# An attention block on one core: cosine product ahead of the block transposition in one step, a set-up product spread over two

## What is computed

```python
xn = layernorm(x)
# attention of xn, with its own norm h = layernorm(xn) * scale + bias
c_q, c_kv = h @ w_down_q.T, h @ w_down_kv.T            # latents, 64 wide
q, k = rope(heads(c_q @ w_up_q.T)), rope(heads(c_kv @ w_up_k.T))
v = heads(c_kv @ w_up_v.T)
attn = softmax(q @ k.T / 8)
a = merge(attn @ v) @ w_out.T + xn
# spiking feed-forward part of xn
y = square(relu(xn @ W_fc.T)) @ W_proj.T
f = (number of 5 leaky integrate-and-fire steps in which y makes the neuron fire) / 5
out = x + a + f
```

## Time and profile before

| | us |
|---|---|
| median of 3 runs | 1083.32 (1083.18 to 1086.99) |
| profiled execution, its own time | 1083.63 |
| its span, first to last instruction | 1081.8 |
| mean granted TensorE clock | 0.993 of full |
| busy: TensorE matmul | 1041.4 (96%) |
| busy: ScalarE | 930.0 (86%) |
| busy: VectorE | 898.9 (83%) |
| busy: GpSimd | 895.9 (83%) |
| DMA engines, mean busy share | 76% |

### The profile page before, as it was taken

The page is one execution under the profiler, slowest core; times in us unless marked ns, Lnnn a source line. Parts: engine busy times, 40 slices in busy tenths (PEclk is TensorE's granted clock), DMA queues, the critical chain, the costliest instruction groups (busy, mean ns, idle before and its releaser), DMA issues.

```text
span 1081.8 us, 26191 instructions
## 1 busy us (share of the span) xinstructions
PE 1041.4 (96%) x6880; PEld 700.7 (65%) x6880; DVE 898.9 (83%) x1223; ACT 930.0 (86%) x3136; POOL 895.9 (83%) x897
## 2 busy tenths in 40 slices
PE   3789999999999999999999999999999999999987
PEld 2556666666666666666666666666666666666654
DVE  3798888898888889888889888889888888888872
ACT  3789988988998888999898999898899889898861
POOL 3777989888888888888898888988888988888851
PEclk9899999999999999999999999999999999999999
DMA  5388777877877877777887777787777787777773
GB/s 178 106 227 207 204 209 202 223 211 200 205 208 204 230 203 207 206 202 202 219 215 207 203 203 209 201 228 208 199 208 206 203 229 204 210 195 196 207 193 81
DMA packets 93281, 217.96 MB, mean 201 GB/s; under 512 B 22464, under 2 KB 43200, under 8 KB 93120
## 3 DMA queue, kind: packets, MB, share of 16 engines
q1 hardware_dynamic: 92864, 216.52, 75.5%
q10 hardware_dynamic: 384, 1.05, 0.4%
HBM read 7.77 MB, written 4.19 MB: 11 GB/s over the span
## 4 chain that ended last, share of the span: by engine, by line
PE 80%; issue 6%; DVE 6%; SPq 3%; ACT 2%; DMA 2%; ACTq 0%; DVEq 0%; POOL 0%; POOLq 0%
PE ps_s L328 20%; PE ps_u L342 20%; PE ps_b L447 10%; PE ps_qk L318 8%; PE ps_a L383 5%; PE ps_a L396 5%; PE ps_qk L319 4%; SPq L254 3%; PE ps_b L413 2%; DVE turned L703 2%; DVE qk L687 2%; PE ps_a L355 1%; PE ps_a L360 1%; PE ps_b L456 1%; PE ps_a L367 1%
## 5 line engine op out<-in xcount | busy, mean ns | idle before, releaser
L538 ACT ACTIVATE prob<-ps_s,neg_max 128x256 f32<-128x256 f32 x1024 | 475.0, 486 | 41.0 <-DVE neg_max L692 38.2
L837 POOL TENSOR_TENSOR partner<-partner,rope_sb 128x512 f32<-128x512 f32 x256 | 327.1, 1278 | 108.3 <-DMA partner<-raw 108.3
L692 DVE TENSOR_REDUCE neg_max<-ps_s 128x4 f32<-128x1024 f32 x256 | 310.8, 1214 | 116.9 <-PE ps_s L328 115.4
L840 POOL TENSOR_TENSOR qk<-qk,partner 128x512 f32<-128x512 f32 x256 | 326.5, 1275 | 20.1
L703 DVE STREAM_TRANSPOSE turned<-prob 128x1024 f32<-128x1024 f32 x256 | 316.4, 1236 | 2.3 <-ACT prob L538 1.3
L328 PE MATMUL ps_s<-qk 64*128 64x256 f32 x2048 | 292.4, 404 | 3.5 <-ACT prob L538 2.4
L342 PE MATMUL ps_u<-gathered,ckv 128*64 128x256 f32 x2048 | 278.4, 393 | 3.1 <-DMA gathered<-turned 2.8
L328 PEld LDWEIGHTS ps_s<-qk 64*128 64x128 f32 x2048 | 177.5, 187 | 106.0 <-issue 86.5
L538 ACT ACTIVATION_READ_ACCUMULATOR prob<-ps_s,neg_max 128x1 f32 x1024 | 221.8, 217 | 0.0
L550 ACT COPY raw<-ps_qk 128x512 f32<-128x512 f32 x256 | 154.1, 602 | 67.0 <-PE ps_qk L319 66.9
L342 PEld LDWEIGHTS ps_u<-gathered,ckv 128*64 128x64 f32 x2048 | 124.8, 136 | 107.8 <-issue 52.6
(11 more groups left out here) (67 smaller groups left out, 897.5 us busy)
## 6 DMA issues: line engine op xcount, KB each, us to landing
gathered<-turned SPq DMA_DIRECT2D x1016, 128.0 KB, 2.4
partner<-raw SPq DMA_DIRECT2D x256, 256.0 KB, 2.4
x_sb<-in_x SPq DMA_DIRECT2D x32, 128.0 KB, 2.3
resid<-early SPq DMA_DIRECT2D x32, 128.0 KB, 2.0
out<-out_sb SPq DMA_DIRECT2D x32, 128.0 KB, 2.1
turned<-in_wup SPq DMA_DIRECT2D x2, 512.0 KB, 5.7
gathered<-turned ACTq DMA_DIRECT2D x8, 128.0 KB, 4.0
rope_sb<-in_rope SPq DMA_DIRECT2D x1, 512.0 KB, 6.8
```

The lines of the kernel that those rows point to most:

```text
L538: last = nc.scalar.activation(prob[:, s % 2, :, h, :, t, :].rearrange("p j k c -> p k j c"), ps_s[:, s % 2, h, t, :].rearrange("p (k j c) ...
L692: nc.vector.tensor_reduce(neg_max[:, s % 2, :, :], ps_s[:, s % 2, :, :, :], AXIS_X, ALU.max, negate=True).then_inc(max_ready, 1)
L837: nc.gpsimd.tensor_tensor(other, other, sin_sb, ALU.mult).then_inc(sin_ready, 1)
L840: nc.gpsimd.tensor_tensor(qk[:, s % 4, :, :], qk[:, s % 4, :, :], other, ALU.add).then_inc(rope_done, 1)
```

## The change

VectorE: in the step p = 1 of every batch, and there alone, `rotate` stands in front of `turn`; `split_latents` stays behind both. TensorE: `value_by_output` takes the half as an argument and is called at p = 6 (pairs 0 to 3, into `ps_u`) and at p = 7 (pairs 4 to 7, into `ps_b`) of b = -2, instead of as a whole at p = 7. ScalarE's copy waits for both halves. The instructions are the same in number and form.

```diff
-            def value_by_output():
+            def value_by_output(half):
                 pe.wait_ge(w_later, LATER_LOADED)
-                for half in range(2):
-                    for j in range(PAIRS // 2):
-                        pair = half * PAIRS // 2 + j
-                        for h in range(2):
-                            rows = slice(h * DH, (h + 1) * DH)
-                            last = nc.tensor.matmul((ps_u, ps_b)[half][h * L:(h + 1) * L, j * D:(j + 1) * D],
-                                                    wv_sb[rows, pair, :], wo_sb[rows, pair, :],
-                                                    start=True, stop=True)
+                for j in range(PAIRS // 2):
+                    pair = half * PAIRS // 2 + j
+                    for h in range(2):
+                        rows = slice(h * DH, (h + 1) * DH)
+                        last = nc.tensor.matmul((ps_u, ps_b)[half][h * L:(h + 1) * L, j * D:(j + 1) * D],
+                                                wv_sb[rows, pair, :], wo_sb[rows, pair, :],
+                                                start=True, stop=True)
                 last.then_inc(setup_pe, 1)
...
-                if p == 7 and isinstance(b, int) and b == -2:
-                    value_by_output()
+                if p in (6, 7) and isinstance(b, int) and b == -2:
+                    value_by_output(p - 6)
...
-                act.wait_ge(setup_pe, 1)
+                act.wait_ge(setup_pe, 2)
...
-                if not outside(g + LEAD["turn"], STEPS):
+                if p != 1 and not outside(g + LEAD["turn"], STEPS):
                     turn(g + LEAD["turn"], s + LEAD["turn"], i)
                 if not outside(g + LEAD["project"], STEPS):
                     rotate(g + LEAD["project"], s + LEAD["project"])
+                if p == 1 and not outside(g + LEAD["turn"], STEPS):
+                    turn(g + LEAD["turn"], s + LEAD["turn"], i)
                 if p == 1 and not outside(b + 2, B):
                     split_latents(b + 2, b0)
```

## The result

The changed kernel is slower, as forecast: 1098.11 us median of four runs (1096.35 to 1100.01) against 1083.71 (1083.18 to 1086.99), ratio 1.0127 with a 95% interval of 1.0100 to 1.0153. The profiled execution took 1096.35 us, its span is 1094.5. Lines of VectorE and ScalarE have a number one lower than before (L686 is the cosine product, L702 the transposition, L730 the split of the latents, L549 the copy to `raw`), and so has TensorE's product of the weights (L465), since the diff takes out a line above them.

The account below looks back on a forecast made before the run. TensorE's full queue was taken as the bound. 1083.6 us plus 13.2 (14 even batches x 0.55 = 7.7, 15 odd x 0.37 = 5.5) plus 0 at the start gave 1096.8 us; own range 1091 to 1102, widened to 1086 to 1104.

Parts of the forecast that it names:

- The bound: TensorE's queue, steady part: once a batch L318 stalls 0.14 us; L396, waiting for the split, starts at 0.38 not 0.23.
- The order, steady part: VectorE at p = 1: waiting for the raw copy delays split and L396, 0.55 us even, 0.37 odd; 13.2 us together.
- the product's hold of the queue: VectorE at p = 1: the cosine product holds the queue 0.57 us before the transposition can start.
- The idle time that I gave as a sign: VectorE in front of the cosine product at p = 1: idle 0.59 us (even) and 0.37 us (odd), waiting for raw.
- The split waits for the full transposition: VectorE at p = 1: the split starts only after the transposition's full end, 1.27 us after its start.
- The lower bound: VectorE at p = 1: if split and transposition overlap, delay is 0.11 us smaller per batch; total cost 7.5 us.
- Nothing accumulates, everything behind shifts alike: Steps behind L396: row maximum, exponentials and next product come 0.59 us later, TensorE too, so no further stall.
- The start: Pipeline fill: halves bring scores(0) 1.1 us sooner, the reorder makes the split 1.1 us late; net 0, -1.4 to +1.1.
- The sum: Whole kernel: profiled 1083.6 us plus 13.2 in the steady batches plus 0 in the fill gives 1096.8 us.
- Rival 1: TensorE at L318 and L396: L396 not held by the split, so the projection's stall goes; 1078 us, chance 0.08.
- Rival 2: ScalarE's raw copy: comes earlier once TensorE is later, VectorE waits only some 0.15 us; 1088 us, chance 0.12.
- Rival 3: Projection of p = 3: stalls 0.43 us more because the product of p = 2 is late; 1109 us, chance 0.10.

Follow-up runs that it names:

- third experiment: Against the kernel before: VectorE at p = 1 runs cosine product, split, transposition, weight products in one block; 1097.54 us, ratio 1.0127.

## Why the prediction was right, point by point

- **The bound.** Right: a stall of 0.14 us at L318 and a second gap at L396 behind the split. That L396 hung on the split already was the step that decided, and it held: before and after, L396 starts 0.05 to 0.13 us behind the split's end, and with the split moved forward it stands 0.23 us behind L413, undisturbed (third experiment).
- **The order, steady part.** Right in mechanism and place. Per pair of batches I had 0.55 + 0.37 = 0.92 us, measured are 1.02 to 1.04. TensorE's own distances give the same: L396 is 0.77 and 0.55 us later behind L413, and L318 0.15 and 0.14 us sooner behind the scores, together 1.03. The term that was too small is the product's hold of the queue: an instruction that VectorE starts out of a wait ran 0.69 us and was followed after 0.61 (584.68 - 584.07), where I took 0.57 from a product that had not waited. That is 0.04 us a batch, twice a pair. The idle time that I gave as a sign, 0.59 and 0.37 us, came out as 0.51 and 0.29: it counts from the end of the row maximum, and I had counted from the start of the transposition, which overlaps its end by 0.08 to 0.09. The delay is not touched by it.
- **The split waits for the full transposition.** Right: 585.95 - 584.68 = 1.27 us. The lower bound, with the overlap of 0.08 us, would have missed by 0.11 us a batch. The Trainium skill (VectorE: DVE Perf Modes, Two Vector instructions with no wait between them) says that an instruction whose output starts in another group of 32 partitions than the last output to the same memory is held until all earlier ones have finished. The trace agrees: the split, which writes from partition 64 on first, came 1.27 us behind the start of the transposition with its 1.24 us.
- **Nothing accumulates, everything behind shifts alike.** Right: one step on, L318 stands 590.07 - 589.00 = 1.07 us behind the scores in the changed kernel's timeline, and every pair is the same.
- **The start.** Right for these two executions: the copy 1.04 us sooner for 1.1, the split 0.1 us later for 0. The halves themselves took 1.90 us (21.29 to 23.19) and 1.26 us (25.20 to 26.46), for 1.62 and either 0.97 or 1.62. I had read the 0.97 as the higher clock; the stretch view gives a granted clock of 1.00 for both halves before (24.92 to 26.54 and 26.54 to 27.51), so that rests on the pace alone. This pace differs from one execution to the next: in the traces of this case scores(0) starts at 27.51 to 28.40 us with the products in one block, and at 25.55 to 26.62 with the halves. The kernel before was profiled at the early end of its range, so 1.05 us is near the low end of what the halves give, and that it met my 1.1 is in part luck. The parts alone show both terms, weakly: the order alone is slower than the whole change by 0.0021 in ratio (2.3 us, with intervals that overlap), the halves alone faster than before by 0.001.
- **The sum.** From the first steady split to the last, 995.58 to 1010.13, the changed kernel is 14.55 us late, of which 0.94 us are there at the first (95.59 to 96.53). I had 13.2: short by the product's hold, about 1.2 us, and by 0.3 us in the fill (the second split, 65.20 for 64.89). The span grew by only 12.7. The last stretch gave back 1.85 us; the granted clock there was 0.97 in the profile before and 1.00 in that after (stretch view, the last lines of before and of after, below), so part of it may belong to the two executions profiled and not to the change; the other three runs were 1.4 to 3.7 us above the profiled one. The clock alone does not explain it: the halves alone, with VectorE's order as before, had a granted clock of 1.00 for 70 us behind their last split, and their last stretch took 86.59 us all the same, where the kernel before took 86.22 and the changed one 84.37. I had no term for it, and it stays open. So my 1096.8 stands as near to the profiled 1096.35 by luck, since two errors of opposite sign cancel; the medians lie 14.4 us apart, where I had 13.2.

```profile
1000.00:1082.00 82.00, 71.68 (x444) 46.03 (x442) 49.28 (x66) 46.36 (x155) 43.16 (x40) 0.97 0.62 160
```

```profile
1000.00:1095.00 95.00, 84.49 (x542) 54.50 (x540) 61.88 (x81) 59.82 (x203) 55.05 (x50) 1.00 0.64 165
```

- **The rivals.** Rival 1 asked that L396 is not held by the split; it was. Rival 2 asked that ScalarE's copy comes sooner against TensorE: its end stands 0.10 us before the scores of p = 2 in even batches, before (512.08 to 512.18) and after (584.04 to 584.14), not moved at all. Rival 3 asked for a second stall at p = 3; there was none, though the third experiment shows that this product is next in line.

What was plainly wrong came later, in the experiments: the expectation of 7 us from removing all of VectorE's stalls. It priced one engine's queue and took the next bound, SyncE's queue, to be far off.

## What to carry to other kernels

Before an instruction is moved forward on a full in-order queue, look at when its input comes: if it comes later than the instruction's new turn, the wait is paid by everything behind it, and what was in front had been covering it for nothing. The cure is not the old order but another instruction that is ready to stand in the gap; here the split, whose input was there. And when a stall of some tenths of a microsecond is taken from a saturated engine, look up how much slack each of its other conditions has, the issue queue of the DMAs among them, because the gain ends at the smallest of them.

## What I had not expected of the hardware

- An issue of one of the gathering DMAs (128 KB, 32 partitions) holds SyncE's queue for 7.54 / 12 = 0.63 us, and 1.9 us lie between the end of the last issue and the matmul that waits for it. The twelve of one group take nearly a quarter of a batch's 32 us, and there are two groups in a batch. This queue was 0.08 us from being the bound, while the DMA engines' mean busy share was 0.78. While the twelve are issued the share is 0.93, so the mean says little about these stretches.
- The cosine product ran 0.69 us when it started out of a wait for ScalarE, and 0.65 us when it followed on a transposition. With the split first, where it follows on the split without a wait (timeline, 514.67 us), it ran 0.69 too. So it seems to be what comes of an empty engine, and not of the wait; no run was made for that.
